# A two-layer recurrent kernel on one core: the period is shifted by half, silu is grouped, the convolution becomes products

## The reference

```python
# layer 0
xn = layernorm(x)
s = (q k^T * decay_mask) v                     # retention, chunks of 128 tokens
h = silu(xn @ w1) * (xn @ w2)                  # 128 -> 512, ternary weights
h = gelu(h @ h1); h = gelu(h @ h2)             # 512 -> 512, twice
x = x + s * silu(h @ w3)
# layer 1
xn = layernorm(x)
x_ssm, gate = split(xn @ W_in + b_in)
x_conv = silu(conv(x_ssm, 4 taps over tokens, per feature) + conv_b)
B, C = split(x_conv @ W_x + b_x)               # 16 states
h_t = exp(-exp(A_log)) * h_(t-1) + x_conv_t B_t    # scan over tokens, 128 x 16 states
s = ((C_t . h_t + D x_conv_t) * silu(gate)) @ W_out + b_out
# mixture of depths on xn: the 512 best of 1024 tokens by xn @ w_router
g = xn + (rank < 512) * sigmoid(score) * (gelu_tanh(xn @ W1 + b1) @ W2 + b2)
x = x + s * silu(g)
```

## Time and profile before

| | us |
|---|---|
| median of 3 runs | 657.72 (651.91 to 658.11) |
| profiled execution, its time | 656.67 |
| profiled execution, span from first to last instruction | 654.9 |
| PE busy / DVE busy / POOL busy / ACT busy | 481.8 / 485.2 / 366.9 / 315.2 |
| mean granted TensorE clock | 0.900 of full |

### The profile page before, as it was taken

One profiled execution on the slowest core, in us unless ns is written; L12 is line 12 of the kernel. 1 busy time (PEld: TensorE's weight loads), 2 busy tenths in 40 slices (PEclk: granted clock), 3 DMA queues, 4 the chain that ended last, 5 costly groups with the idle time before them and its releaser, 6 DMA issues.

```text
span 654.9 us, 5965 instructions
## 1 busy us (share of the span) xinstructions
PE 481.8 (74%) x1795; PEld 280.3 (43%) x1795; DVE 485.2 (74%) x751; ACT 315.2 (48%) x482; POOL 366.9 (56%) x380
## 2 busy tenths in 40 slices
PE   1348887788887987697888878788879775675762
PEld 0236654455545553374446544555455432222220
DVE  2530230478789879987888989887899969998974
ACT  3336586557544655376535843566536541332110
POOL 1734453389548664766756764685577546534322
PEclk9989998969897989897997999789979887778875
...
DMA packets 5504, 11.53 MB, mean 18 GB/s; under 512 B 864, under 2 KB 1504, under 8 KB 5216
## 3 DMA queue, kind: packets, MB, share of 16 engines
...
## 4 chain that ended last, share of the span: by engine, by line
PE 35%; DVE 30%; ACT 14%; issue 13%; POOL 5%; DMA 1%; SPq 0%; DVEq 0%; POOLq 0%; ACTq 0%
PE bank0a L792 12%; DVE hs L1149 6%; DVE xbank L1137 5%; PE bank1a L874 4%; DVE plain L1040 2%; ACT plain L536 2%; PE bank1a L848 2%; POOL hidAl L449 2%; POOL hs L463 2%; PE ybank L901 2%; ACT L536 2%; PE bank0a L750 2%; PE xbank L890 2%; ACT L524 2%; ACT fh L524 1%
## 5 line engine op out<-in xcount | busy, mean ns | idle before, releaser
L463 POOL TENSOR_TENSOR hs<-hs,Ct 128x512 f32<-128x512 f32 x128 | 169.4, 1324 | 75.7 <-DVE hs L1149 69.8
L890 PE MATMUL xbank<-xpair,spr 128*128 128x512 f32 x128 | 75.0, 588 | 42.3 <-DVE hs L1149 42.2
L1137 DVE TENSOR_TENSOR xbank<-xbank,Bt 128x512 f32<-128x512 f32 x128 | 88.3, 690 | 17.3 <-PE xbank L890 17.3
L449 POOL TENSOR_TENSOR hidAl<-plain,hidAh 128x512 fp32r<-128x512 f32 x48 | 62.7, 1307 | 56.6 <-ACT hidAh L537 47.6
L449 POOL TENSOR_TENSOR hidBl<-plain,hidBh 128x512 fp32r<-128x512 f32 x48 | 63.0, 1315 | 49.6 <-ACT hidBh L537 46.4
L1149 DVE TENSOR_TENSOR_SCAN hs<-decay,carry,xbank 128x512 f32<-128x512 f32 x64 | 81.7, 1276 | 7.4 <-DVE xbank L1137 0.5
L1149 DVE TENSOR_TENSOR_SCAN hs<-decay,xbank 128x512 f32<-128x512 f32 x64 | 77.8, 1215 | 4.6
L792 PE MATMUL bank0a<-hidAh,hTh 128*128 128x512 f32 x128 | 58.3, 455 | 15.1 <-ACT hidBh L537 14.2
L792 PE MATMUL bank0a<-hidBh,hTh 128*128 128x512 f32 x128 | 60.0, 469 | 8.3 <-ACT hidAh L537 8.1
L890 PEld LDWEIGHTS xbank<-xpair,spr 128*128 128x128 f32 x128 | 26.1, 204 | 93.4 <-DVE hs L1149 67.2
L792 PE MATMUL bank0a<-hidBl,hTh 128*128 128x512 f32 x128 | 53.0, 414 | 0.0
...
## 6 DMA issues: line engine op xcount, KB each, us to landing
...
```

The lines of the kernel that those rows point to most:

```text
L449: pool.tensor_tensor(low[:, m, :], plain[:, k % NPLAIN, :], high[:, m, :].bitcast(F32), ALU.subtract).then_inc(hidden_low, 1)
L463: pool.tensor_tensor(h, h, Ct[:, hs_(u)], ALU.mult).then_inc(p_ready, 1)
L890: pe.matmul(xbank[i % 2][:], spr[:, at, :], xpair[:, half, hs_(u)], start=True, stop=True).then_inc(xs_full, 1)
L1137: dve.tensor_tensor(xbank[i % 2][:], xbank[i % 2][:], Bt[:, hs_(u)], ALU.mult).then_inc(xb_ready, 1)
```

## The change

- Time is counted from the preparation of a unit instead of from its scan. `units(p)` is now e = p-2, t = p-1, n = p, v = p+1, w = p+2, and p goes from -1 to 8, the last with 11 slots. `scanned(p, s)` says which scan step a slot has: from slot 8 of period p on unit p's steps 0 to 7, in slots 0 to 7 of the next period its steps 8 to 15. A unit's norm, projections, convolution, B and C lie in slots 1 to 7 of its period, its scan begins in slot 8.
- The comparisons of unit t lie in slots 3 to 8 (before: 7 to 14), own chunks first; the token weights in slot 9, `gate_y` in 10, `mod_update` in 12, `output` in slot 1 of the period after (units 6 and 7: slots 14 and 9).
- `residual_l0` and `gate_l0` move from slot 15 to slot 0 of the next period; on DVE `residual_l0` stands between `times_b` and `scan`.
- silu is grouped: `gate_l0`, `mod_gate`, the four `z_silu`, `convolved` and `take_gate` come one after the other in slots 0 to 5.
- The convolution is four f32 products on PE with weights W_in * conv_w (`w_conv`, made once on POOL), accumulated in `bank1a`, with narrow products for the first three tokens. The projection "ssm" and DVE's `convolve` go. `conv_biases` makes the bias once on DVE. A parameter of 128x512 is loaded more.
- `score_columns` goes from DVE to ACT, one group a period, `scol` has two buffers. `mod_up` lies in slots 13 to 15 of the preparation, `mod_down` in two halves in slots 10 and 11.
- The additions of epsilon and the sign of the mean go from POOL to DVE (`tensor_scalar` on 128x4) for both norms. `ynT` has 2 buffers instead of 3.
- On POOL the low parts of z come in slots 1 to 4, of h1 in 6 to 9, of h2 in 11 to 14.

```diff
-PERIODS = range(-2, UNITS + 1)
+PERIODS = range(-1, UNITS + 1)
+LEAD = NGRP // 2
...
+    return within(p - 2), within(p - 1), within(p), within(p + 1), within(p + 2, 1)
+def scanned(p, s):
+    u = p if s >= LEAD else p - 1
+    return (u, (s - LEAD) % NGRP) if 0 <= u < UNITS else (None, None)
+def after(p, s):
+    return (p, s + 1) if s < NGRP - 1 else (p + 1, 0)
+def slots(p):
+    return range(NGRP if p < UNITS else LEAD + 3)
+def chunk_at(u, pos):
+    own = u % 2 * CPH
+    return own + pos if pos < CPH else (own + pos) % CH
+def compare_slots(u):
+    return (0, 0, 1, 1, 2, 2, 3, 3) if u == UNITS - 1 else (3, 4, 4, 5, 7, 8, 8, 8)
 def weights_slot(u):
-    return 10 if u == UNITS - 1 else 15
+    return 5 if u == UNITS - 1 else 9
+def update_slot(u):
+    return 6 if u == UNITS - 1 else 12
...
     if _v is not None:
...
+        L0_ACT += [("z1", _v, 0), ("z1", _v, 1)]
+        L0_DVE += [("z2", _v, _m) for _m in range(KT)]
     if _n is not None:
         L0_ACT.append(("tok", _n))
+        L1_ACT += [(_k, _n) for _k in ("xnT", "score", "conv", "gate", "score_col", "B", "C")]
+        L1_ACT += [("ffn", _n, _m) for _m in range(KT)]
     if _v is not None:
...
+        L0_ACT += [("z1", _v, 2), ("z1", _v, 3)] + [("h1", _v, _m) for _m in range(KT)] + [("u", _v), ("h2", _v, 0)]
     if _w is not None:
...
+        L0_ACT.append(("xnT", _w))
         L0_DVE += [("scores", _w), ("outer", _w)]
     if _v is not None:
...
+        L0_ACT.append(("h2", _v, 1))
+    if _w is not None:
+        L0_ACT.append(("q", _w))
+    if _v is not None:
+        L0_ACT += [("h2", _v, 2), ("h2", _v, 3), ("w3", _v)]
         L0_DVE.append(("s", _v))
...
+    if _t is not None:
+        L1_DVE += [("rank", _t), ("ffn", _t), ("out", _t)]
 HIDDEN = [(k, t, m) for t in range(UNITS) for k in ("z", "h1", "h2") for m in range(KT)]
...
+            pool.wait_ge(l1_params, 16 * NPARAM_L1)
+            pool.tensor_tensor(w_conv[:], lw[:, 0:P].rearrange("p (o d) -> p o d", o=1).broadcast_to([P, TAPS, P]),
+                               raw_conv, ALU.mult).then_inc(w_conv_ready, 1)
             for p in PERIODS:
...
                 take1(("score", t), srow[:, hs_(t)])
+            def score_columns(t):
+                act.wait_ge(l1_act_full, done(L1_ACT, ("score_col", t)))
+                act.activation(scol[:, t // 2 % 2, cs_(t)], bank1a[:].rearrange("p (c i) -> p c i", i=P)[:, :, 0],
+                               ACT.Copy).then_inc(l1_act_done, 1)
...
             def take_gate(t):
+                take1(("gate", t), gate[:, hs_(t)], ACT.Silu, bias=scale("b_in", 1))
+            def convolved(t):
+                if t == 0:
+                    act.wait_ge(b_conv_step, 5)
+                    act.wait_ge(w_conv_ready, 1)
                 if t >= 2:
                     act.wait_ge(yg_ready, t - 1)
...
+                take1(("conv", t), xc[:, hs_(t)], ACT.Silu, bias=b_conv[:, 0:1])
+                act.wait_ge(l1_act_done, done(L1_ACT, ("conv", t)))
                 for half in range(2):
                     rows = slice(half * P // 2, (half + 1) * P // 2)
                     last = act.activation(xpair[rows, half, hs_(t)], xc[rows, hs_(t)], ACT.Copy)
                 last.then_inc(x_high, 1)
...
+            def slot(p, s):
+                e, t, n, v, w = units(p)
+                if n is not None and s == 0:
+                    gate_l0(n)
+                if s == 0 and e is not None and e != UNITS - 2:
+                    mod_gate(e)
+                if v is not None:
+                    if 1 <= s < 1 + KT:
+                        z_round(v, s - 1)
+                    if s < KT:
+                        z_silu(v, s)
                 if n is not None:
...
+                    if s == 1:
                         to_tokens(n)
...
+                    elif s == 2:
                         norm_l1(n)
...
+                    elif s == 3:
                         take1(("xnT", n), ynT[:, n % NYNT, :])
...
+                    elif s == 4:
                         take_scores(n)
...
+                    elif s == 5:
+                        convolved(n)
+                        take_gate(n)
+                if v is not None and s == 5:
+                    hidden("h1", v, 0)
+                if n is not None:
+                    if s == 6:
+                        score_columns(n)
+                        take_B(n)
+                    elif s == 7:
+                        take_C(n)
+                if v is not None and 6 <= s < 5 + KT:
+                    hidden("h1", v, s - 5)
+                if n is not None and n % 2 == 1 and s == 7:
+                    sigmoid_half(n // 2)
+                if w is not None and s == 8:
                     norm_l0(w)
                 if v is not None:
...
+                    if s == 9:
                         take_u(v)
...
+                    if 10 <= s < 10 + KT:
+                        hidden("h2", v, s - 10)
                 if w is not None:
...
+                    if s == 10:
                         retention_in(w)
...
+                    elif s == 11:
                         retention_q(w)
                 if n is not None:
...
+                    if s == 14:
+                        mod_up(n, 0)
+                        mod_up(n, 1)
+                    elif s == 15:
+                        mod_up(n, 2)
+                        mod_up(n, 3)
+                if t is not None and t >= UNITS - 2 and s == update_slot(t) + 1:
...
                     pe.matmul(bank[:], w, ynT[:, t % NYNT, :], start=True, stop=True).then_inc(l1_act_full, 1)
+                def convolve(t, taps):
+                    if TAPS - 1 in taps:
+                        open1a(("conv", t))
+                        pe.wait_ge(l1_act_done, done(L1_ACT, ("xnT", t)))
+                        if t == 0:
+                            pe.wait_ge(w_conv_ready, 1)
+                            pe.wait_ge(b_conv_step, 5)
+                    for k in taps:
+                        s = TAPS - 1 - k
+                        if s > 0 and t % 2 == 1:
+                            pe.matmul(bank1a[:, 0:s], w_conv[:, k, :], ynT[:, (t - 1) % NYNT, HALF - s:HALF],
+                                      start=False, stop=False)
+                        last = pe.matmul(bank1a[:, s:HALF], w_conv[:, k, :], ynT[:, t % NYNT, 0:HALF - s],
+                                         start=(s == 0), stop=(k == 0))
+                        if s == 0 and t % 2 == 0:
+                            pe.matmul(bank1a[:, 0:TAPS - 1], ident[:], b_edge[:], start=False, stop=False)
+                    if 0 in taps:
+                        last.then_inc(l1_act_full, 1)
                 def project_x(job, t, w):
...
                     pe.matmul(bank[:], w, xc[:, hs_(t)], start=True, stop=True).then_inc(l1_act_full, 1)
                 def score_column(t):
-                    bank = open1d(("score_col", t))
+                    bank = open1a(("score_col", t))
                     pe.wait_ge(l1_act_done, done(L1_ACT, ("score", t)))
                     for j, c in enumerate(chunks(t)):
                         last = pe.transpose(bank[:, ck(j)], srow[:, ck(c)], ident[:])
...
+                def slot(p, s):
+                    e, t, n, v, w = units(p)
+                    u, k = scanned(p, s)
+                    u_next, k_next = scanned(*after(p, s))
+                    if u_next is not None:
+                        spread_x(u_next, k_next)
+                    if t is not None:
+                        for pos in range(CH):
+                            if compare_slots(t)[pos] + 1 == s:
+                                rank(t, pos)
+                    if v is not None and s < KT:
+                        z1(v, s)
+                    if s == 0 and t is not None:
+                        gather_y(t, 1)
+                    if v is not None and s < KT:
+                        z2(v, s)
                     if n is not None:
...
+                        if s == 1:
                             to_tokens(n)
...
+                        elif s == 3:
                             norm_to_features(n)
...
+                        elif s == 4:
                             project("score", n, W_R)
...
+                    if s == 4 and t is not None:
+                        gather_y(t, 2)
+                    if n is not None:
+                        if s == 4:
+                            convolve(n, (3, 2, 1, 0))
+                        elif s == 5:
+                            project("gate", n, W_IN[:, P:2 * P])
+                        elif s == 6:
+                            project_x("B", n, W_B)
+                    if v is not None and 5 <= s < 5 + KT:
+                        hidden("h1", v, s - 5)
+                    if n is not None:
+                        if s == 5:
+                            score_column(n)
+                        elif s == 6:
+                            project_x("C", n, W_C)
```

(66 more changed lines are left out.)

338 lines of the change are left out of this document (86 added, 252 removed).

## The result

The changed kernel takes 668.82 us (median of four runs, 664.56 to 671.0), the kernel before 657.91 beside it; the ratio is 1.0176, 95% interval 1.0128 to 1.0223. It is slower by 1.8%. The forecast was 617 with a range of 600 to 646: sign and size were wrong. The profiled execution has a span of 666.5 us against 654.9.

A forecast was written before the change was run, and what follows sets the result against it. DVE and PE share the bound in full periods, DVE idles in the head and works alone at the end; 129.5 + 5 * 66.0 + (65.9 - 3.5) + 52.5 + 29 + 11.2 = 614.6 span, forecast 617, range 600 to 646.

The forecast's parts named there:

- Slot 4: PE's peak of 5.8 us (score, gather, four convolution products) would be covered by DVE's 9.3 us of work.
- DVE's slots 0 to 9: Sum of DVE's work in slots 0 to 9 of a full period: 37.2 us of 54.6.
- at nothing: POOL loses four small operations, about 1 us of 46.7 a period; having slack, this was counted as no gain.
- Slots 10 to 15: PE leads in a period's last six slots: 23.3 us, 25 at 0.93 clock, 27.4 with three turns with ACT.
- Convolution as products: In a full period DVE loses net 3.7 us and PE gets 3.0, of which 1 counts.
- PE pays: Rival: PE's added 3.0 us lengthen each full period; 638 if in part (0.16), 657 if in full (0.07).
- PE has room: Rival: added products are free on PE, full periods fall to 63 us or below; 599 in all, chance 0.08.
- Table loads: ACT's five loads a period become three, saving 2.6 us, of which half, 1.3, was counted.
- The head: Up to period 1: first scan at about 102 us, period 0 takes 52.5, period 1 begins at 129.5.
- Period 7, period 8, tail: The end, after the full periods: 52.5 us, 29 us and an unchanged tail of 11.2.
- The slower rival: The residual in front of slot 0's scan makes DVE wait, 8 to 9 us a period; about 670, chance 0.06.
- periods of 69 us or more: Sign of being wrong in the six full periods; then look at DVE's spread waits in slots 5 to 7, 10 to 15.

The follow-up runs named there:

- a1_rank: Changed kernel with slot 4's rank product moved behind the convolution in PE's queue: 647.66 us, ratio 0.9867.
- a4: Changed kernel with the score column moved from slot 5 to slot 4, ahead of the convolution: 658.86 us, ratio 1.0053.
- c1_rank_col: Changed kernel with both reorderings, rank product behind the convolution and score column ahead of it: 643.98 us, ratio 0.9794.
- p_half: c1_rank_col with POOL weighing only half the columns of each state by C: 624.31 us, ratio 0.952.
- c4_dve: c1_rank_col with the convolution back on DVE, as a projection and four instructions in slot 4: 661.01 us, ratio 1.0118.
- b_prod: Kernel before with the convolution as products on PE and `ynT` in two buffers, order unchanged: 659.22 us, ratio 1.0045.
- c3_conv1: c1_rank_col with only one of the convolution's four products, narrow ones left out: 641.01 us, ratio 0.9774.
- d2_gelu: c6_bal with `mod_up` computed by the exact gelu's table, so one table load falls away: 635.25 us, ratio 0.9684.
- b_gelu: Kernel before with gelu in place of silu for gate and convolution, two table loads fewer a period: 633.34 us, ratio 0.9663.
- c6_bal: c5_ret with `mod_down` in slots 2 and 3, last four comparisons and w's statistics a slot later, sigmoid by unit: 641.57 us, ratio 0.9789.
- d3_up1: c6_bal with only the first of four `mod_up` products and activations made: 602.25 us, ratio 0.9182.
- c2_head: c1_rank_col with two groups of h1 issued ahead of the score in period 0: 649.45 us, ratio 0.985.
- a2_conv1: Changed kernel with one convolution product issued in place of four, narrow ones left out: 643.79 us, ratio 0.9817.
- a3_res: Changed kernel with `residual_l0` behind the scan of slot 0 instead of in front: 666.18 us, ratio 1.0138.
- c5_ret: c1_rank_col with `retention_out` and its copy in slots 3 and 4 instead of slot 9: 643.02 us, ratio 0.9798.

## Why the prediction was wrong

- **Slot 4, the step that failed.** "PE is one slot ahead there and DVE has 9.3 us of work before it needs the spread behind that peak, so it is covered." PE cannot be ahead of a product that needs the comparison of the slot before. The rank product binds PE's slot 4 to the end of DVE's slot 3, and everything behind it in the queue with it, the peak included. The change moved comparisons to slots 3 and 4, in front of the convolution; I priced the moved comparisons by their durations ("cost the same where they are") and not by the wait that each puts on PE's queue. Shown by a1_rank: 21 us (21.7 in slots 0 to 9, 3.6 a period for a wait of 3.0; of the 21.7, 14.8 are idle time of DVE and 6.9 its shorter instructions).
- **DVE's slots 0 to 9, mis-sized.** I summed 37.2 us from means of the kernel before. In the changed kernel the comparisons have 1073 ns in the place of 669, 32 * 0.404 = 12.9 us, the second step of `output` 8 * 0.43 = 3.5; others became shorter. Of the 34.4 us, 22.4 are the order in slot 4 (a1 and a4 together, 262.4 - 240.0), and a part of those 12.9 goes with them: the mean is 807 in c1_rank_col. Of the 12.0 left, 7.2 are busy time of DVE above my sum (230.4 for 6 * 37.2 = 223.2) and 4.8 idle time. I put POOL "at nothing" for its slack; p_half shows that its instructions lengthen DVE's. That slots 0 to 9 of p_half come to 228.0 like my forecast is chance: DVE is busy 215.5 in them, not 223.2, and my means had POOL's full work in them.
- **Slots 10 to 15, right**, 27.6 a period for 27.4, the turns with ACT included, though at a granted clock of 1.00 where I had 0.93. The sum of PE's pitches has a slip, 27.3 + 23.3 = 50.6 and not 51.6; nothing in the forecast uses the difference.
- **Convolution as products, right in this order**: net 2.6 us a period (c4_dve) where I had 3.7 - 1 = 2.7. "PE pays" holds for the old order alone (b_prod). "PE has room" fell as a forecast (71.3 us a period for 63); its premise, that the added products are nearly free, holds once slot 4 is put right: three of them are worth 3 us by the medians (c3_conv1).
- **Table loads.** I counted half of 2.6 us. What a load is worth hangs on what else ends beside it: nothing in d2_gelu's full periods, at most 23 us for the two loads a period in b_gelu, the shorter chain behind the convolution included. By the rule of the Trainium skill, "ScalarE: Activation LUTs", section "What ACT_TABLE_LOAD costs", with its drain, it was to be 8 us more; the earlier trace rows and c6_bal (344.32 + 1.28 = 345.60, the next activation at 345.61) show no drain behind the 1.28.
- **The head, wrong by 14.9.** The first scan came at 109.55 where I had 102, 7.5 late; slots 8 to 15 of period 0 took 34.8 where I had 27.5, 7.3 more. For the second, c6_bal and d3_up1 differ there by 35.1 - 29.3 = 5.8: I had counted the four `mod_up` of period 0 by their products and not by their turns. For the first, PE works at a mean clock of 0.84 up to the first scan, where I had counted its products at full clock; score and convolution alone last 8.4 us, for the most part at the lower level. c2_head excludes h1's place and a2_conv1 the number of the convolution's products. That the clock makes up the 7.5 us is argued: no run changed it by itself.
- **Period 7, period 8, tail, right** to 0.7 and 0.8.
- **The slower rival** named the wrong mechanism: moving the residual changes the median by 2.6 us, not clear of noise (a3_res). That its 670 lies 1 us from the measured 668.8 is chance. The sign of being wrong that I had named, periods of 69 us or more, did come (71.3), and slots 5 to 7, which it names, are among those that lasted too long. That the kernel got slower by a wait put in PE's queue was none of my cases.

Of the complete kernels that were run, c6_bal (641.57), c5_ret (643.02) and c1_rank_col (643.98) are the fastest, 2.0 to 2.1% below the kernel before; their intervals overlap. A second bank for `mod_up`, which might end the turns that d3_up1 prices, wasn't tried.
